# A decoder block on one core: the order of loads and of row sends in the mixing stage

## The reference

```python
def _mha(x, ...):                  # x is taken as (S=8, B=512, D): attention over the 8 sequences at one position
    qkv = x @ Wqkv.T + bqkv ; 4 heads of 64 ; softmax(q k^T / 8) v ; @ Wo.T + bo
def _moe(x, ...):                  # 8 experts, D=256, DF=1024
    idx = argmax(x @ Wg.T) ; each row goes to its one expert: relu(x W1[e] + b1[e]) @ W2[e] + b2[e]
x = _layernorm(x)
y = _layer_norm(x + _mha(x), g1, be1)
z = _layer_norm(y + _moe(y), g2, be2)
out = residual + z
```

## Time and profile before

| | |
|---|---|
| median of three runs | 1191.25 us |
| profiled execution | 1189.84 us, span 1187.8 us |
| PE, DVE, ACT, POOL busy over the span | 93%, 62%, 40%, 43% |
| DMA, mean over the span | 116 GB/s |
| attention / mixing / experts, from the timelines | 0 to 687 / 688 to 887 / 887 to 1187.8 us |

### The profile page before, as it was taken

One profiled execution on the slowest core, in us unless ns is written; L12 is line 12 of the kernel. 1 busy time (PEld: TensorE's weight loads), 2 busy tenths in 40 slices (PEclk: granted clock), 3 DMA queues, 4 the chain that ended last, 5 costly groups with the idle time before them and its releaser, 6 DMA issues. The chain is left out here.

```text
span 1187.8 us, 29501 instructions
## 1 busy us (share of the span) xinstructions
PE 1103.9 (93%) x10067; PEld 746.0 (63%) x10068; DVE 741.6 (62%) x2088; ACT 478.3 (40%) x866; POOL 509.4 (43%) x758
## 2 busy tenths in 40 slices
PE   9989999999999999999989899899879999999995
PEld 3546455465464554644644455656649999999994
DVE  4645776667757766677544535788755566555663
ACT  5435545454545454545354223333213333333330
POOL 3325425335245253352342032454544565666554
PEclk9999999999999999999999999999999999999998
DMA  7272563744544637445475236454212111111110
GB/s 223 65 207 72 150 190 102 195 122 132 172 121 122 185 103 200 112 119 167 110 181 157 66 122 168 149 174 129 90 52 90 46 45 49 52 52 56 51 42 7
DMA packets 143477, 137.95 MB, mean 116 GB/s; under 512 B 30376, under 2 KB 136750, under 8 KB 143280
## 3 DMA queue, kind: packets, MB, share of 16 engines
q1 hardware_dynamic: 137808, 124.20, 37.1%
q0 software_dynamic: 5280, 12.66, 3.3%
q10 hardware_dynamic: 320, 0.16, 0.1%
HBM read 49.38 MB, written 50.83 MB: 84 GB/s over the span
## 5 line engine op out<-in xcount | busy, mean ns | idle before, releaser
L976 ACT ACTIVATE probs<-ps_ab 128x512 f32<-128x512 f32 (+2 forms) x352 | 174.5, 538 | 94.8 <-PE ps_ab L1298 38.8
L597 POOL TENSOR_SCALAR_AFFINE_SELECT probs<-probs 128x512 f32<-128x512 f32 x128 | 81.6, 637 | 269.1 <-ACT probs L976 265.9
L2887 PE MATMUL ps_ab<-e_yT,e_w_now 128*128 128x128 f32 x1248 | 147.9, 277 | 0.0
L2887 PEld LDWEIGHTS ps_ab<-e_yT,e_w_now 128*128 128x128 f32 x1248 | 144.6, 194 | 0.5 <-ACT e_yT L2858 0.4
L2898 PE MATMUL ps_c<-keep_w,e_hT 128*128 x624 | 141.0, 379 | 0.0
L2898 PEld LDWEIGHTS ps_c<-keep_w,e_hT 128*128 128x128 f32 x624 | 115.7, 190 | 14.1
L718 DVE CUSTOM_DVE_ANT_0 ps_ab<-ps_ab,mask_qk 128x256 f32<-128x256 f32 x224 | 89.0, 451 | 18.8 <-PE ps_ab L1267 18.7
L712 DVE TENSOR_REDUCE top<-ps_ab 128x2 f32<-128x512 f32 (+1 forms) x112 | 74.2, 684 | 31.1 <-PE ps_ab L1267 30.3
L1829 ACT ACTIVATE e_w_now<-keep_w 128x1024 f32 x78 | 78.1, 1049 | 37.0 <-issue 37.0
L2822 DVE TENSOR_SCALAR e_hT<-ps_ab,keep_b 128x128 f32<-128x128 f32 x312 | 84.4, 343 | 10.0 <-PE ps_ab L2887 7.4
L1267 PE MATMUL ps_ab<-k_rows,q_rows 96*128 96x256 bf16 (+1 forms) x512 | 85.0, 261 | 4.6 <-DVE top L718 2.7
(11 more groups left out here) (250 smaller groups left out, 2131.3 us busy)
## 6 DMA issues: line engine op xcount, KB each, us to landing
sorted_rows<-filler SPq DMA_DIRECT2D x8, 4290.0 KB, 17.0
q_rows<-parts SPq DMA_DIRECT2D x96, 128.0 KB, 2.4
k_rows<-parts SPq DMA_DIRECT2D x96, 128.0 KB, 2.4
q_rows<-q_parts SPq DMA_DIRECT2D x96, 128.0 KB, 2.4
keep_w<-in_e_w SPq DMA_DIRECT2D x16, 512.0 KB
keep_w<-in_e_w SPq DMA_DIRECT2D x8, 1024.0 KB
e_row<-sorted_rows SPq DMA_DIRECT2D x39, 130.0 KB, 2.1
x_in<-in_x SPq DMA_DIRECT2D x8, 512.0 KB, 4.0
```

The costliest lines, as they stand in the source:

```text
L597: nc.gpsimd.affine_select(own, own, [[0, TILES], [1, P]], ALU.is_ge, keep_zero, base=0, channel_multiplier=-1).then_inc(probs_cut.sem, 1)
L976: nc.scalar.activation(probs[:, user % 2, lo:lo + width], ps_exp[:, f % 2, 0:width], ACT.Exp).then_inc(exp_done.sem, 1)
L2887: mm = nc.tensor.matmul(ps_h[s][:, f // 4, (f % 4) * P:(f % 4 + 1) * P], w1_now[:, s, k, f * P:(f + 1) * P], yT[:, s, k * P:(k + 1) * P], ...
```

## The change

The first part is in SP's stream. Before, each round issued an expert's weights first, then the next group's rows; the weights waited for the scores (`scores_full`), and the rows were behind them. Now the weights of expert n+1 wait for the transposed features (`xT_ready`) and the rows of group n+3 are issued right behind them, when the normalisation of group n+2 is done. For the same group the wait on `ln_done` is the same (count(n, 3*TILES) is count(n+2, TILES)); what differs is which expert's weights lie in front of the rows. The second part is in POOL's stream: `send_rows(n - 1)` stands behind `iteration(n)` and no longer ahead of it.

```diff
@@ block.sync
                 sp.wait_ge(ln_done.sem, ln_done.count(0, TILES))
                 load_x(1)
-                sp.wait_ge(xT_ready.sem, xT_ready.next(-1, KD))
-                load_expert(0)
-                for n in range(NGROUPS - 1):
-                    sp.wait_ge(scores_full.sem, scores_full.count(n, 1))
+                for n in range(-1, NGROUPS - 1):
+                    sp.wait_ge(xT_ready.sem, xT_ready.next(n, KD))
                     load_expert(n + 1)
-                    if n < NGROUPS - 2:
-                        sp.wait_ge(ln_done.sem, ln_done.count(n + 1, TILES))
-                        load_x(n + 2)
+                    if n < NGROUPS - 3:
+                        sp.wait_ge(ln_done.sem, ln_done.count(n, 3 * TILES))
+                        load_x(n + 3)
@@ block.gpsimd
                 for n in range(2, NGROUPS):
+                    iteration(n, ahead=n < NGROUPS - 1, more=n < NGROUPS - 2)
                     send_rows(n - 1)
-                    iteration(n, ahead=n < NGROUPS - 1, more=n < NGROUPS - 2)
                 send_rows(NGROUPS - 1, (0, 1))
                 iteration(NGROUPS, ahead=False, more=False)
```

## The result

The changed kernel was slower. In its first timing it took 1206.91 us (median of 4, 1204.85 to 1211.76) against 1190.55 for the kernel before, timed beside it: ratio 1.0137, 95% interval 1.0115 to 1.016. In three later timings of the same text, on chips 1, 7 and 15, the ratio was 1.0053 (1.0035 to 1.0071), 1.0037 (1.0016 to 1.0058) and 1.0022 (1.0002 to 1.0041). The forecast was 1189.7 us, 1.55 us faster. So sign and size were wrong, and a part of the size, about 11 of the first 16 us, did not come back in any later timing.

What follows compares the result with a forecast made beforehand. The prediction took PE's restart in each round as the bound, and POOL at the mixing stage's end. Terms -2.1 - 2.24 + 2.8 = -1.55 us took 1191.25 to 1189.7 us, own range 1187.5 to 1192.

Steps and rivals of the forecast that it cites:

- Rows of group 2 earlier: Round 0 to 1: PE goes straight on to the output projection; gain 2.1 us, bounds 1.58 and 2.4.
- Rows of groups 3 to 7 earlier: Rounds 1 to 3: rows go out some 1.4 us earlier, without 2 MB in front; DVE's three shorter waits go.
- Sends a group later: Rounds 2 to 5: DVE pays 0.95 us a round, not 3.03; rounds fall to PE's 19.55; gain 2.24, bounds 0 and 2.4.
- Six sends ahead of the last root: End of the mixing stage: POOL's last root starts at 870.0, not 867.25; loss 2.8 us, bounds 2.4 and 4.5.
- PE idle for 4 to 5 us ahead of the choice: Sign expected in the profile after, near the mixing stage's end; about 4.7 us of idling instead of 1.9.
- Rival A: Experts' start: PE idles longer, clock falls, filler runs longer, no pause precedes the experts; sum -4.0, 1187.3 us; chance 0.22.
- Rival B: Mixing rounds: bias steps still hold DVE 3.03 us a round, so rounds do not speed up; -0.6, 1190.6 us; chance 0.14.
- Rival C: Filler before the experts: at half clock it ends 4.7 us past their start; +3.2, 1194.4 us, slower; chance 0.07.
- Rival D: Round 0 to 1: group 2's rows land no earlier, behind expert 0's weights; +0.5, 1191.8 us; chance 0.07.

Runs made afterwards that it cites:

- kernel 12: The changed kernel a fourth time, nothing edited, on one more chip: 1192.59 us, ratio 1.0022 to the kernel before.
- kernel 8: The changed kernel a third time, nothing edited, on one chip with its two halves: 1193.04 us, ratio 1.0037 to the kernel before.
- kernel 10: The changed kernel with its sends put behind the bias halves, early in the round: 1186.47 us, ratio 0.9976 to the kernel before.
- kernel 9: The kernel before with only the new order of loads, POOL's sends as before, second timing: 1184.70 us, ratio 0.9961.
- kernel 1: The kernel before with only the new order of loads, POOL's sends as before, first timing: 1182.57 us, ratio 0.9932.
- kernel 5: The changed kernel again, word for word: 1192.91 us, ratio 1.0053 to the kernel before.
- kernel 7: The changed kernel with group 6 sent ahead of the last full iteration, as before the change: 1192.25 us, ratio 1.0037 to the kernel before.

## Why the prediction was wrong

**Rows of group 2 earlier: right in mechanism, somewhat large in size.** The forecast was an output projection right behind the transposes, 2.1 us sooner. With the new loads it comes within 0.3 us of them in every profile. The stretch to restart 1 fell from 41.29 to 37.75 us, 3.54; but 1.70 of that is the stage's first q and k projections, 8.83 us in the kernel before's profile (granted clock 0.88 from 690 to 704 us) and in kernel 12's, 7.13 in all others (1.00 in the first of the changed kernel), which the loads have no part in. That leaves 1.84 us. Against the two profiles of the sends alone, whose loads are the old ones (39.04 and 38.23 us), it is 1.3 and 0.5, under the forecast's lower bound of 1.58. Part of the term is paid back at once: the loads now lie beside the scores of groups 0 and 1, 1.51 and 1.43 us where they were 1.29.

**Rows of groups 3 to 7 earlier: right.** The three shorter waits are gone.

**Sends a group later: the failed step.** It rested on "Its four sends run in what was idle time". POOL was idle there, but PE was not, and the statement was never tested against PE. What it says of DVE came out: keep_gate at 0.85 us, and DVE 4.4 to 5.1 us ahead of the end of the stretched scores in the first profile. What PE does then was forecast at 19.55 us a round and was 20.4 to 23.3 in kernel 8 and 23.4 to 25.4 in the first profile (rounds 2 to 5). Where the sends are taken away from the scores, the term as worked out is there: 19.44 to 19.57 us in kernel 10. So the working for rounds was right for a PE whose own pace is constant, and the change altered that pace. In the sum this term stood at -2.24 us for four rounds. From the output projection of round 2 to that of round 6 the kernel before took 80.44 us, the first profile of the changed kernel 97.22 and kernel 8 86.72: +16.8 and +6.3 us.

The other half of the term, the 3.03 us a round that DVE was to save, is no fixed price either. keep_gate's 3.18 us began at 774.94, 0.35 us into the fourth send (774.59) and ahead of the bias steps. In kernel 9 it began at the same 0.35 us into that send and took 0.14:

```profile
772.13 0.96 POOL L2125 DMA_INDIRECT sorted_rows<-m_rows,m_slot  x1 [0.30 <-issue]
772.48 0.14 DVE L2235 TENSOR_TENSOR m_xnb<-m_v,m_gate_sums 128x32 f32<-128x32 f32 x1
```

Kernel 1, the same text in another loading, had 3.19 us in rounds 3 to 6 like the kernel before. So the blocking is real where it comes, but one profile does not say that it always comes.

**Six sends ahead of the last root: right.** Forecast 8.2 us from the last number step to the root and a wait of about 5 us; measured:

```profile
878.22 0.23 POOL L2118 TENSOR_SCALAR m_token<-m_token 128x4 f32<-128x4 f32 x1 [0.20 <-POOL m_rows L2116]
879.09 1.10 POOL L2125 DMA_INDIRECT sorted_rows<-m_rows,m_slot  x1 [0.65 <-issue]
...
886.55 0.20 POOL L2090 TENSOR_TENSOR m_veps<-m_moments,m_eps 128x2 f32<-128x2 f32 x1
...
887.60 0.88 DVE L2259 SCALAR_TENSOR_TENSOR m_rows<-m_mixed,m_rstd,m_be 128x256 f32<-128x256 f32 x2 [4.92 <-POOL m_rstd L2092]
```

8.1 us, from the end of the step at 878.45 to 886.55, and 4.9 us. From the end of the scores to the experts, the changed kernel on one chip takes 39.99 us and its load half 37.56, and kernels 5 and 7 differ by 3.1: 2.4 and 3.1 us for a term of 2.8. (The first column of the table has 39.72 for the kernel before because its own round 7 lost time: an output projection of 5.49 us where the others have 3.84, behind a pause of 1.34, and then the products with v in pieces.) One sign missed: PE idle for 4 to 5 us ahead of the choice. It was 3.2 us, and 3.1 in kernel 8, because the filler matmuls ahead of it also came later: in kernel 8 they start 0.7 us later behind the scores than in kernel 9, and take 0.7 us longer.

**Rival A came true in the wrong kernel.** "The experts start at full clock": in kernels 1, 9 and 10 the 36 filler matmuls lengthen and the first expert matmuls are at full pace. PE's timeline of kernel 9:

```profile
873.80 0.17 PE L2592 MATMUL ps_d<-m_chosen,m_before 128*128 128x16 bf16 x1 [2.06 <-DVE m_chosen L2277]
...
876.10 9.26 PE L2536 MATMUL ps_c<-m_before,m_ident 128*128 128x512 bf16 x36
886.84 0.68 PE L2908 MATMUL ps_c<-m_identf 128*128 128x128 f32 x4 [1.49 <-PEq L2022]
...
888.21 3.84 PE L2885 MATMUL ps_ab<-e_yT,e_w_now 128*128 128x128 f32 x32
```

3.84 us for what took 5.93 before. Its granted clock was 0.85 from 874 to 876 and 0.84 from 876 to 885, and 1.00 from 885 to 895. The second half of the rival's chain is there: the clock is lower, the filler ends later, and the pause ahead of the experts shrinks from 3.17 to 1.49 us. Its first half is not: the clock was to fall because PE idles longer, and PE idled 2.06 us here against 1.92 before, where the clock held. Why it fell is open. It may be a part of why the load half is faster than the waits alone suggest. In kernel 8, where PE did idle longer (3.07 us), the filler took 8.88 us and the pause was 1.82 us, yet the first 32 took 5.40 us.

**Rivals B, C and D** did not decide: keep_gate was short, the filler did not reach past the experts' start, the rows came in time. None of them touched the place that failed, and the slower rival (C) was in the wrong stage.

**Open.** Why the first timing was 1.4% slower and three others 0.2 to 0.5%. All its executions on record, 21, lie between 1203.68 and 1211.76 us, so it was no stray run, and the kernel before was normal beside it. Its profile has the same stretch at twice the size, even where no x_in load stands beside the scores. It came with one chip or one loading of the program, and nothing run here tells these apart. One row leans to the chip: the kernel before, another program, has its products of round 7 in pieces and at 2.61 us in its profile, and no kernel measured later is over 2.02. Open too is what PE lacks in the pauses. The trace names no releaser, and the packets of the instruction queue took 0.9 to 1.5 us before and after alike. Unlike the single long pauses, the pieces do not start with such a packet: in round 2 of kernel 8 none starts between 3.9 us before the scores and 1.5 us into them. A path that PE's instructions share with POOL's transfers would fit, and is argued, not shown.

## What to carry to other kernels

An engine's idle time is free only if what is put there leaves the others their pace. Before moving indirect transfers, look at what TensorE does in those microseconds: beside large matmuls they cost PE nothing here, beside 128 matmuls of about 10 ns each they cost 0.5 us, and 1.2 to 2.2 us when other loads were issued at the same time. Look for a place where the profile already has the two side by side; here round 7 of the kernel before had it. Try the halves of a change apart: here the loads alone were worth 0.4 to 0.7%, and the sends took that and 0.2 to 0.5% more.

## What the runs showed of the hardware

- Small matmuls do not always keep their pace beside other engines' transfers. 128 of them in 1.29 us is the pace alone; beside POOL's indirect transfers 1.8, beside these and SP's row loads 2.5 to 3.5, in the first profile up to 4.6 us, with pieces of 1 to 6 matmuls in them, mostly some 0.75 us apart.
- Single long pauses of PE (0.62 to 2.41 us, 17 in 15 profiles, at three places of the program) end 1.25 to 1.56 us after a 16 KB packet of the instruction queue has ended. At the two places in the scores they are absent where that packet started 2.8 us or more ahead of them. A wait for instructions fits this; no run tests it.
- A stretched block can bring the clock down to 1.2 GHz behind it. Behind the 4.58 us of round 2 the output projection took 5.99 us, and behind the 2.96 us of kernel 8 it took 6.09; behind 2.84 and 2.90 in the same kernel it stayed at 3.79. The Trainium skill, "TensorE: Matmul & The Clock Gate", section "Why this matters for your kernels", warns of idle gaps between bursts of matmuls. The trace agrees that a long gap can bring the clock down (0.53 granted behind the 3.17 us ahead of the experts), but here it took no long one: from the start of round 2's scores to those 5.99 us the longest pause is 1.05 us.
- The same program differed by 1.2% between chips or loadings, while the kernel before stayed within 0.4% on them. The first timing alone would have overstated the loss of the later ones at least threefold.
